# Two graph layers on one Trainium2 core: a scratch memset behind each slot's gathers, with POOL waiting for its own write

## The reference, cut to what matters

```
h   = layernorm(x) @ W                      # 6250 x 8 heads x 32
e   = leaky_relu(a_src[src] + a_dst[dst])   # one logit per edge and head; layer 0 adds an edge term
w   = softmax of e over the edges of one destination
out = segment_sum(h[src] * w, dst) + bias   # the sum over each node's incoming edges
```

## Time and profile before

| what | us |
| --- | --- |
| median of 3 timed runs | 6676.67 (6676.18 to 6681.97) |
| span of the profiled execution, its own time | 7807.0 |
| PE busy in it | 5257.7 |
| POOL busy in it | 3613.4 |
| DVE busy in it | 3278.9 |
| ACT busy in it | 1371.0 |

### The profile page before, as it was taken

One profiled execution on the slowest core, in us unless ns is written; L12 is line 12 of the kernel. 1 busy time (PEld: TensorE's weight loads), 2 busy tenths in 40 slices (PEclk: granted clock), 3 DMA queues, 4 the chain that ended last, 5 costly groups with the idle time before them and its releaser, 6 DMA issues. The chain is left out here.

```text
span 7807.0 us, 99204 instructions
## 1 busy us (share of the span) xinstructions
PE 5257.7 (67%) x19729; PEld 3739.4 (48%) x19729; DVE 3278.9 (42%) x5938; ACT 1371.0 (18%) x2977; POOL 3613.4 (46%) x3708
## 2 busy tenths in 40 slices
PE   2387887788788878228999625556565556663498
PEld 1144444444444444227999514444444444442498
DVE  6255555555555555721111313333333333336244
ACT  2122222222222222002222200000000000000122
POOL 2635555555555554042222056666666666650222
PEclk9689999999999999658999857777777777786699
DMA  6434444444444443515666544444444444434255
GB/s 220 136 101 122 122 119 123 124 124 125 122 123 121 122 124 102 186 60 165 183 183 183 153 102 114 113 115 115 114 112 113 113 114 116 113 102 154 101 198 188
DMA packets 718013, 1022.24 MB, mean 131 GB/s; under 512 B 301733, under 2 KB 531561, under 8 KB 692608
## 3 DMA queue, kind: packets, MB, share of 16 engines
q0 software_dynamic: 183456, 485.95, 23.8%
q1 hardware_dynamic: 527676, 519.31, 21.7%
q10 hardware_dynamic: 6564, 14.14, 0.5%
HBM read 868.26 MB, written 153.27 MB: 131 GB/s over the span
## 5 line engine op out<-in xcount | busy, mean ns | idle before, releaser
L773 POOL DMA_INDIRECT e_rows<-sc_table,e_eidx x3224 | 3115.9, 966 | 2253.8 <-issue 952.6
L880 PE MATMUL e_ps_o<-e_rows,e_oh 128*128 128x264 f32 x6448 | 1918.5, 449 | 856.9 <-ACT e_res L969 700.8
L880 PEld LDWEIGHTS e_ps_o<-e_rows,e_oh 128*128 128x128 f32 x6448 | 1379.2, 222 | 1384.3 <-issue 1147.6
L1064 DVE SCALAR_TENSOR_TENSOR e_u<-e_encr,e_adst,e_ps_hd 128x512 f32<-128x512 f32 x806 | 597.1, 745 | 1160.2 <-remote 366.1
L1132 DVE TENSOR_TENSOR e_rows<-e_rows,e_ps_w 128x1024 f32<-128x1024 f32 x806 | 970.7, 1207 | 106.3 <-issue 83.5
L822 PE MATMUL e_ps_X<-e_u,e_hwide 128*104 128x512 f32 x1612 | 871.1, 635 | 16.8 <-DVE e_u L1064 14.8
L1055 DVE TENSOR_SCALAR e_ohT<-e_at,e_nid 96x512 bf16<-96x512 int16 x806 | 292.5, 363 | 1384.6 <-DMA e_aw<-sc_a2p 553.7
L969 ACT COPY e_res<-e_ps_o 32x264 f32<-32x264 f32 x806 | 296.0, 367 | 3291.4 <-PE e_ps_o L884 1242.4
L810 PE MATMUL e_ps_enc<-e_at,e_w_enc 96*128 96x512 bf16 x806 | 317.9, 394 | 570.6 <-ACT e_encr L942 383.4
L1676 PE MATMUL x_ps_h<-x_xT,x_w 128*128 128x256 f32 x2624 | 648.2, 405 | 15.4 <-DMA x_b<-in_L_ffn_b_dram 15.4
L1676 PEld LDWEIGHTS x_ps_h<-x_xT,x_w 128*128 128x128 f32 x2624 | 638.5, 337 | 20.6 <-issue 16.4
(11 more groups left out here) (290 smaller groups left out, 3538.7 us busy)
## 6 DMA issues: line engine op xcount, KB each, us to landing
x_w<-in_L_ffn_W_dram SPq DMA_DIRECT2D x112, 1024.0 KB
e_at<-sc_grp SPq DMA_DIRECT2D x403, 192.0 KB
x_w<-in_L_ffn_w_dram SPq DMA_DIRECT2D x60, 1024.0 KB
e_rows<-sc_table,e_eidx POOLq DMA_INDIRECT x3224
e_at<-sc_grp SPq DMA_DIRECT2D x403, 96.0 KB
sc_agg<-e_res SPq DMA_DIRECT2D x816, 33.0 KB
sc_xb<-r_zero SPq DMA_DIRECT2D x24, 1032.0 KB
x_xin<-sc_xb SPq DMA_DIRECT2D x86, 258.0 KB
```

What stands on the lines that cost most here:

```text
L773: pool.indirect_dma_start(rows[:, k, s, j, :], None, dr["table"][:, :], bass.IndirectOffsetOnAxis(eidx[:, k, s, j:j + 1], 0)).then_inc(s_r ...
L880: nc.tensor.matmul(ps_o[:, 0:ROW], oh[:, k, at_j:at_j + P], rows[:, k, s, j, :], start=(j == 0), stop=False)
L1064: nc.vector.scalar_tensor_tensor(u[:, p, h, :], encr[:, h, :], adst[:, h:h + 1], ps_hd[:, h, :], ALU.add, ALU.mult).then_inc(s_u, 1)
```

## The change

Behind the four gathers of each slot POOL writes a scratch row of 1 x 128 numbers, `rest`, with a memset, which raises a new semaphore `s_rest`; then it waits for `s_rest` to count that memset, before it goes on. `gather` gets the batch number as an argument, since the count runs over all slots. Nothing reads `rest`.

```diff
+        rest = sb("rest", [1, 128], F32)
...
+        s_rest = sem("rest")
...
-            def gather(k, s):
+            def gather(b, k, s):
                 for j in range(CH):
                     pool.indirect_dma_start(rows[:, k, s, j, :], None, dr["table"][:, :],
                                             bass.IndirectOffsetOnAxis(eidx[:, k, s, j:j + 1], 0)).then_inc(s_rows[k], 16)
+                nc.gpsimd.memset(rest[:, :], 0.0).then_inc(s_rest, 1)
+                hold(pool, s_rest, b * SB + (s + 1), s_pg)
...
-                    gather(k, s)
+                    gather(k, k, s)
...
                     hold(pool, s_o, b * SB + (O0 + s + 1), s_pg)
-                    gather(k, s)
+                    gather(b + 2, k, s)
```

## The result

The changed kernel takes 7321.43 us (median of 4 runs, 7318.8 to 7324.8) against 6676.43 us before: ratio 1.0966, with a 95% interval of 1.0952 to 1.0979. That is 645 us more; the prediction said 614 more and 7291 us, so the forecast held. Three of its steps did not (the first stage being POOL's, the number of slots, and the gaps once a turn of the loop), and their errors nearly cancelled.

The account below looks back on a forecast made before the run. The prediction took POOL's unbroken gathers to bound both edge stages in a timed run. 767 slots at 0.80 us gave 614 us, and 6676.67 + 614 = 7291 us, range 6850 to 7480.

Parts of the forecast that it names:

- the first stage being POOL's: First edge stage: nearly level between POOL and PE-ACT before; at 5.8 us a slot against 5.05, it becomes POOL's.
- the number of slots: Both edge stages: slots that pay the price, 754 from first total to last gather plus 13 ahead, 767.
- the gaps once a turn of the loop: POOL's loop in the edge stages: the prediction had no term for them, only 0.80 us for each of 767 slots.
- the 1130 us: Profile span 7807.0 us less timed 6676.67: taken as waits in the edge stages that only the profiled execution has.
- POOL gathers without a break in both edge stages: In a timed run POOL has no gap and sets both edge stages' length, 3793.7 us in all.
- The sum that carried it: Whole kernel: 2884.9 us outside the edge stretches plus POOL's chain of 3793.7 gives 6678.6, against 6676.67 timed.
- The slot of 5.05 us: First edge stage: PE-ACT's slot, between two ACT L969 copies in undisturbed slots, against POOL's 5.0 us.
- The price C: Time added between a slot's fourth gather and the next first one: 0.80 us taken, ends 0.05 and 1.06.
- The cheap wait: Rival: the gather is made ready behind the memset, C 0.05 to 0.5, giving 6715 to 7060 us; chance 0.15.
- Not slower: Rival: timed runs have the profile's room, 1.8 and 1.2 us a slot; 6680 us, chance 0.06; faster, 6560, 0.03.
- PE as a further bound: Rival: PE waits longer each slot and its granted clock falls; 7440 to 7600 us; chance 0.10.
- The weighing of the memset against the compare: Memset beside DVE's compare: passes; if held like the gather, one of 13 slots pays up to 0.75, 44 us.

Follow-up runs that it names:

- the second trace: The kernel before, unchanged, profiled once more: span 6677.4 us.
- the disturbed trace: The first profiled execution of the kernel before, unchanged: span 7807.0 us, against timed runs of 6676.
- the two-memset run: Two memset-and-wait pairs behind each slot's four gathers, where the changed kernel has one: 7617.65 us, ratio 1.1411 to the kernel before.
- the kernel with the late wait: The changed kernel, but each slot waits for the memset of the slot before, with two scratch rows in turn: 6704.11 us, ratio 1.0038 to the kernel before.
- three gathers: Each slot's fourth gather left out: of the kernel before, 6248.58 us (ratio 0.9359); with the change's memset and wait, 6534.23 us (0.9791).

## Why the prediction was right, and which of its steps were wrong

**That the 1130 us belonged to one execution** was right: the second trace spans 6677.4 us. **"POOL gathers without a break in both edge stages"** was right for the second and wrong for the first. The sum that carried it, 6678.6 us, came out right by chance. It took the 2884.9 us outside the two stretches from the disturbed trace as if they were undisturbed, and gave the stretches POOL's 3793.7. In the second trace the same gathers span 2069.6 and 1867.9 us, 3937.5 together, 144 more than that, most of it in the first stage; and outside them lie 2739.9 us, 145 less (the first gather behind a total comes at 376.25, not 470.24). The slot of 5.05 us for the first stage was the other half of the mistake: it was a slot without the once-a-batch work, and PE is busy 68.4 us a batch (1916 / 28), 5.3 a slot.

**The price C**, 0.80, measured 0.84. Its three pieces were 0 + 0.20 + 0.86 - 0.30 and came out 0 + 0.19 + 0.95 - 0.30. Taking the rows in which a DMA stands behind a wait, and not those in which a compute instruction does, was the choice that made the forecast; the two-memset run shows both side by side, 0.15 and 0.95. The Trainium skill, "Perfetto Trace Analysis", per-engine timelines, has such a DMA pushed into a wait queue while the sequencer goes on; by that reading C would have been near 0.05. In the loop it is a register instruction that waits, so the rule is not put to the test there. At a stage's start the gather itself waits, and it started 0.79 us after the memset's end, which speaks against that reading. Where the wait does not stall, in the kernel with the late wait, C was 0.05. The shares of C are not what the pieces suggest: the memset alone costs 0.06.

**The number of slots**, 767, should have been 806. The disturbed trace had POOL idle for 97.21 us behind the first two batches of the first stage; undisturbed, POOL runs straight through from them to the next batch in both stages, and ACT's copy of the source logits waits for gathers in both stages after the change, 62 times instead of 33. First the wait's row before, then after:

```profile
ACT e_alog L946 <- DMA e_rows<-sc_table,e_eidx: 665.8, 33, 88.3
```

```profile
ACT e_alog L950 <- DMA e_rows<-sc_table,e_eidx: 1273.7, 62, 97.1
```

**The sum, as measured.** From the start of a stage to batch 2, 18.5 us more in each (26 slots, about 0.7 each). Behind it 377 slots at 0.84 are 316.7 us a stage. In the second stage come 14 x 2.5 = 35 on top: of the 2.5 us a turn 1.4 are the uncovered halt (a mean of 2.04 instead of 0.65) and 0.7 the longer gaps at the first gathers of its two batches (1.47 and 1.14 instead of 0.95), the rest is in small differences. That makes 370; measured from first to last gather, 370.6. In the first stage the halt was there before, so only the 0.7 a turn, 10 us, come on top, and the 70 us that POOL had waited for PE are taken back: 18.5 + 316.7 + 10 - 70 = 275; measured 272.0. With 3 us elsewhere, 645. The prediction had 390 slots x 0.80 = 312 for the second stage, 59 too little, and 377 x 0.80 = 302 for the first, 30 too much. So the missing slots, the gaps once a turn and the 0.04 in C (about +100 in all) were set off by the missing room of the first stage (-70), and the 31 us between 614 and 645 are what is left. The size of C is the part that was worked out; that the total came this close is in part luck.

**Rivals.** The cheap wait fell with the timeline. "Not slower" fell; its mechanism, room under PE, is real in the first stage, and with three gathers it hides the whole price there, but in the changed kernel it was worth 70 us. PE as a further bound did not come, though its first sign did: the granted clock fell from 0.98 to 0.93 and from 0.84 to 0.79, but PE's busy time stayed within 26 us in either stretch. The weighing of the memset against the compare came out small: no memset took over 0.378 us. The gather beside the compare is another matter, 2.26 us in the row above. The Trainium skill, "SBUF — State Buffer", on the two separate sides, lets a DVE instruction with two SBUF inputs hold up a GpSimd instruction that reads SBUF. The trace agrees, if a gather counts as one for its indices, which the code keeps in SBUF; with one input in PSUM it took 0.95. No run here moved the indices.

## What to carry to other kernels

On POOL a stalled wait just ahead of an indirect DMA cost 0.8 us here, though what it waited for took 0.2; the same wait on something already done cost nothing. So where the order allows it, put such a wait one slot later. A profile whose span is far from the timed runs should be taken again before anything is read from its idle times: the busy times of DVE, ACT and POOL agree here within 1% between the two traces, but PE's is 8% longer in the disturbed one, and the waits and the starts of the stages are far off. And whether an engine bounds a stage is told more surely by taking a quarter of its work away than by its busy share.

## What was not expected of the hardware

- A 1x128 memset between two gathers is nearly free: it fits in the 0.30 us between them (0.35 with it).
- POOL halts once a turn of the loop, for 2.04 us ahead of one gather. In the second stage this showed in full in none of 14 turns before the change, and in all 14 with a stalled wait shortly ahead.
- With two SBUF inputs, DVE's compare of 1.88 us lengthens a gather beside it from 0.95 to 2.26 us; with one of them in PSUM it does not.
- One profiled execution was 17% longer than every timed run, and the next profiled one of the same kernel was not.
